# Fewer chunks scattered whole, and every third node one-hot on ScalarE, in a graph update with two segment sums

## What is computed

```python
in_agg = segment_sum(edge_feat, dst, 6250)          # edge_feat: 200000 x 64
out_agg = segment_sum(edge_feat, src, 6250)
h = relu(concatenate([in_agg, out_agg, x], 1) @ W1 + b1)   # W1: 192 x 256
out = layernorm(x + h @ W2 + b2)                    # W2: 256 x 64
```

## Time and profile before

| | |
|---|---|
| median of 3 runs | 1354.76 us (1354.26 to 1355.96) |
| profiled execution | 1358.4 us |
| its span, first to last instruction | 1356.6 us |
| mean granted TensorE clock | 0.942 |
| busy: PE, weight load, DVE, ACT, POOL | 83%, 68%, 86%, 68%, 80% of the span |
| scatters (L775) | 628, 1.673 us mean |
| node one-hots on DVE, on ACT | 1300, 260 |

### The profile page before, as it was taken

One profiled execution on the slowest core, in us unless ns is written; L12 is line 12 of the kernel. 1 busy time (PEld: TensorE's weight loads), 2 busy tenths in 40 slices (PEclk: granted clock), 3 DMA queues, 4 the chain that ended last, 5 costly groups with the idle time before them and its releaser, 6 DMA issues.

```text
span 1356.6 us, 60124 instructions
## 1 busy us (share of the span) xinstructions
PE 1129.9 (83%) x21795; PEld 917.9 (68%) x21795; DVE 1167.1 (86%) x3489; ACT 926.2 (68%) x2047; POOL 1084.1 (80%) x663
## 2 busy tenths in 40 slices
PE   2667588988898888898888889989888898899596
PEld 2546377877787777787777767767666676777443
DVE  6756689988999999998899989999879898999486
ACT  6233588988898888888788876666566676666242
POOL 3888888888888888888888888888888888888533
PEclk9976789999999999999899989999989998999798
DMA  9332489999998899998999998889878887888441
GB/s 300 49 43 17 62 182 209 212 195 199 203 215 203 200 202 205 209 210 199 207 235 243 241 217 210 199 209 216 212 166 209 192 200 188 185 195 207 79 133 45
DMA packets 251312, 247.53 MB, mean 182 GB/s; under 512 B 105587, under 2 KB 213460, under 8 KB 250966
## 3 DMA queue, kind: packets, MB, share of 16 engines
q1 hardware_dynamic: 158632, 216.16, 52.4%
q0 software_dynamic: 92384, 28.77, 27.8%
q10 hardware_dynamic: 144, 0.48, 0.1%
HBM read 139.12 MB, written 106.21 MB: 181 GB/s over the span
## 4 chain that ended last, share of the span: by engine, by line
POOL 33%; DMA 26%; issue 23%; PE 11%; DVE 4%; ACT 2%; SPq 1%; POOLq 0%; ACTq 0%; DVEq 0%
POOL out_tables L775 32%; DMA out_tables<-payload,target 23%; PE psum L1679 3%; DMA feat<-in_edge_attr 2%; PE psum L1890 2%; PE psum L1845 1%; PE psum L1902 1%; PE psum L1655 1%; ACT slots_out L870 1%; DMA rows_i<-in_dst 1%; PE psum L1618 1%; DVE same L1357 1%; PE psum L1628 0%; ACT parts L849 0%; ACT payload L887 0%
## 5 line engine op out<-in xcount | busy, mean ns | idle before, releaser
L775 POOL DMA_INDIRECT out_tables<-payload,target x628 | 1050.7, 1673 | 209.4 <-issue 170.0
L1679 PE MATMUL psum<-parts,to_slot 128*128 128x194 bf16 x4524 | 457.9, 251 | 88.7 <-ACT slots_out L870 75.0
L1679 PEld LDWEIGHTS psum<-parts,to_slot 128*128 128x128 bf16 x4524 | 377.9, 99 | 136.1 <-ACT slots_out L870 92.6
L870 ACT ACTIVATE slots_out<-psum 128x388 bf16<-128x388 f32 x780 | 341.7, 499 | 68.4 <-PE psum L1679 54.2
L1703 PE MATMUL psum<-to_node,slots_in 64*64 64x313 bf16 x9360 | 353.3, 301 | 24.6 <-issue 19.9
L1703 PEld LDWEIGHTS psum<-to_node,slots_in 64*64 64x64 bf16 x9360 | 278.2, 108 | 85.4 <-issue 33.4
L1291 DVE TENSOR_SCALAR to_slot<-iota_h,slot 128x480 bf16<-128x480 f16 (+1 forms) x936 | 291.3, 367 | 29.6 <-PE psum L1679 29.1
L1330 DVE TENSOR_SCALAR to_node<-iota_h,slot_rel 128x318 bf16<-128x318 f16 x780 | 239.7, 329 | 0.0
L1330 DVE TENSOR_SCALAR to_node<-iota_rows,slot_rel 128x318 bf16<-128x318 f16 x520 | 181.8, 350 | 0.0
L887 ACT ACTIVATE payload<-psum 128x256 f32<-128x256 f32 x157 | 58.9, 375 | 159.5 <-PE psum L1757 87.1
L937 ACT ACTIVATE apart<-iota_h,slot_rel 128x318 bf16<-128x318 f16 x260 | 131.9, 551 | 12.0 <-DVE slot_rel L1302 10.3
(11 more groups left out here) (138 smaller groups left out, 894.6 us busy)
## 6 DMA issues: line engine op xcount, KB each, us to landing
slot_tiles<-slots_out SPq DMA_DIRECT2D x156, 388.0 KB
feat<-in_edge_attr SPq DMA_DIRECT2D x195, 256.0 KB
slots_in<-slot_tiles SPq DMA_DIRECT2D x152, 242.5 KB
slots_in<-slot_tiles SPq DMA_DIRECT2D x152, 230.4 KB
slot_tiles<-slots_out SPq DMA_DIRECT2D x78, 194.0 KB
out_tables<-payload,target POOLq DMA_INDIRECT x628
out_tables<-zeros POOLq DMA_DIRECT2D x4, 1600.0 KB
feat<-out_tables SPq DMA_DIRECT2D x48, 128.0 KB, 2.3
```

The source lines that it names most:

```text
L775: e.indirect_dma_start(out_tab, at, payload[b][:, t, :], None, element_offset=k * TABLE_ROWS * D, compute_op=ALU.add).then_inc(s_tab[k], 16)
L870: e.activation(slots_out[b][:, g:g + n, m, :], round_bank(b, r)[:, 0:n * SLOT_W].rearrange("p (g w) -> p g w", w=SLOT_W), ACT.Copy).then_i ...
L1679: last = e.matmul(round_bank(b, r)[:, o:o + SLOT_W], to_slot[m][:, COLUMN_FROM[k] + t * P:COLUMN_FROM[k] + (t + 1) * P], parts[b][:, SHARE ...
```

## The change

- SUMS 16 to 14: 80 chunks are shared, 14 go whole after them; 160 tiles per node pair, 1600 in all. The units 1 to 12 have 118.3 tiles each, the last has 160.
- ROUND 6 to 3: tiles 2, 5, 8, ... are ACT's. Its second pass (`from_far`) covers two tiles, whose `to_node` buffers are three apart, in one instruction; APARTS 4.
- `slots_in` in a ring of 6 parts of 16 tiles, PARTS = 10, no longer a multiple of the ring.
- In the summing units the targets of the first quad are worked out apart, after quad 1's "same node", so that POOL can start on them.
- `in_group` in six pieces, one per k, each waiting for the one before.

```diff
-SUMS = 16
+SUMS = 14
...
-RING = 4
-PARTS = 2 * RING
+RING = 6
+PARTS = 10
...
-ROUND = 6
+ROUND = 3
 BY_SCALAR = 1
 BY_VECTOR = ROUND - BY_SCALAR
-APARTS = 2
+APARTS = 4
...
-            return isinstance(c, int) and c in (0, END_SHARE)
+            return isinstance(c, int) and (c == 0 or END_SHARE <= c < N_CHUNKS)
...
+        def ring_buf(g, p):
+            return (g * PARTS + p) % RING
...
-            def from_far(g, i):
-                n = scalar_rounds(tile_no(g, i)) - 1
-                e.wait_ge(s_apart, n + 1)
-
-                e.wait_ge(s_tile, tile_no(g, i) + 1)
-                e.activation(to_node[:, node_buf(g, i), :], apart[:, n % APARTS, :], ACT.Relu, bias=1.0,
-                             scale=-1.0).then_inc(s_to_node_act, 1)
+            def from_far(tiles):
+                first, last = tiles[0], tiles[-1]
+                n = scalar_rounds(tile_no(*first)) - 1
+                e.wait_ge(s_apart, n + len(tiles))
+
+                e.wait_ge(s_tile, tile_no(*last) + 1)
+                e.activation(to_node[:, node_buf(*first):node_buf(*last) + 1:ROUND, :], apart[:, n % APARTS:n % APARTS + len(tiles), :],
+                             ACT.Relu, bias=1.0, scale=-1.0).then_inc(s_to_node_act, len(tiles))
...
-                    for k in range(0, len(mine), APARTS):
-                        for at in mine[k:k + APARTS]:
-                            to_far(*at)
-                        for at in mine[k:k + APARTS]:
-                            from_far(*at)
+                    pairs = []
+                    for at in mine:
+                        odd = (scalar_rounds(tile_no(*at)) - 1) % 2
+                        if odd and pairs and len(pairs[-1]) == 1 and not at[1] < pairs[-1][0][1]:
+                            pairs[-1].append(at)
+                        else:
+                            pairs.append([at])
+                    for k in range(0, len(pairs), APARTS // 2):
+                        for pair in pairs[k:k + APARTS // 2]:
+                            for at in pair:
+                                to_far(*at)
+                        for pair in pairs[k:k + APARTS // 2]:
+                            from_far(pair)
...
-                step(e.tensor_tensor(in_group[:, :, :, :], from_group[:, :, 0:SLOT_GROUPS, :], from_group[:, :, 1:, :],
-                                     ALU.subtract))
+                for k in range(MINI):
+                    last = e.tensor_tensor(in_group[:, k, :, :], from_group[:, k, 0:SLOT_GROUPS, :], from_group[:, k, 1:, :],
+                                           ALU.subtract)
+                    if k < MINI - 1:
+                        last.then_inc(s_in_group, 1)
+                        e.wait_ge(s_in_group, (MINI - 1) * n + k + 1)
+                step(last)
...
                     if q == 1:
                         for h in range(HALVES):
                             add_window(c, b, ats, h)
+                        targets(c, b, c, mode, (0, QUAD))
...
-                        targets(c, b, c, mode)
+                        targets(c, b, c, mode, (QUAD, mode.cols))
```

More of the change, by code:

```diff
@@ L326, in build @@
         s_from_group = sem("s_from_group")
+        s_in_group = sem("s_in_group")
         s_masked = sem("s_masked")
@@ L445, in targets_no @@
                 return c + 1 + (1 if c > 0 else 0)
-            return c + (2 if mode is SHARING else 3)
+            if mode is SHARING:
+                return c + 2
+            return c + 2 + (c - END_SHARE if mode.sums else SUMS)
         def quad_buf(q, b, mode):
@@ L622, in load_tiles @@
                 lo = PART_FROM[p]
-                into = slots_in[p % RING][:, a - lo:z - lo, :].rearrange("p t w -> p (t w)")
+                into = slots_in[ring_buf(g, p)][:, a - lo:z - lo, :].rearrange("p t w -> p (t w)")
                 homes = slot_rows[0:HOME_AT[MINI], :].rearrange("(k r) w -> r k w", k=MINI)
@@ L627, in load_tiles @@
                     e.dma_start(into[j:P:LOADS, :], homes[both * g:both * (g + 1), 2 * j:2 * j + 2, a * SLOT_W:z * SLOT_W]
-                                ).then_inc(s_slot_in[p % RING], 16)
+                                ).then_inc(s_slot_in[ring_buf(g, p)], 16)
                 at = HOME_AT[MINI] + shared * g
                 e.dma_start(into[LOADS - 1:P:LOADS, :], slot_rows[at:at + shared, a * SLOT_W:z * SLOT_W]
-                            ).then_inc(s_slot_in[p % RING], 16)
+                            ).then_inc(s_slot_in[ring_buf(g, p)], 16)
             def load_part(g, p):
@@ L936, in to_far @@
                 k = i - PART_FROM[p]
-                e.activation(apart[:, n % APARTS, :], iota_h[:, 0:HOT], ACT.Abs, bias=slot_rel[p % RING][:, k:k + 1],
+                e.activation(apart[:, n % APARTS, :], iota_h[:, 0:HOT], ACT.Abs, bias=slot_rel[ring_buf(g, p)][:, k:k + 1],
                              scale=-1.0).then_inc(s_apart, 1)
-            def from_far(g, i):
-                n = scalar_rounds(tile_no(g, i)) - 1
-                e.wait_ge(s_apart, n + 1)
-                e.wait_ge(s_tile, tile_no(g, i) + 1)
-                e.activation(to_node[:, node_buf(g, i), :], apart[:, n % APARTS, :], ACT.Relu, bias=1.0,
-                             scale=-1.0).then_inc(s_to_node_act, 1)
+            def from_far(tiles):
[5 more added lines that the diff above has]
+                             ACT.Relu, bias=1.0, scale=-1.0).then_inc(s_to_node_act, len(tiles))
             def tiles_to_nodes(u, q):
@@ L1297, in relative @@
             def relative(g, p):
-                e.wait_ge(s_slot_in[p % RING], 16 * LOADS * (g * (PARTS // RING) + p // RING + PIECES))
+                e.wait_ge(s_slot_in[ring_buf(g, p)], 16 * LOADS * ((g * PARTS + p) // RING + PIECES))
                 e.nop(nofuse=True)
                 n = PART_FROM[p + 1] - PART_FROM[p]
-                e.scalar_tensor_tensor(slot_rel[p % RING][:, 0:n], slots_in[p % RING][:, 0:n, 3 * D],
-                                       pair_first[:, bass.ds(g, 1)], slots_in[p % RING][:, 0:n, 3 * D + 1],
+                e.scalar_tensor_tensor(slot_rel[ring_buf(g, p)][:, 0:n], slots_in[ring_buf(g, p)][:, 0:n, 3 * D],
+                                       pair_first[:, bass.ds(g, 1)], slots_in[ring_buf(g, p)][:, 0:n, 3 * D + 1],
                                        ALU.subtract, ALU.add).then_inc(s_slot_rel, 1)
@@ L1329, in tiles_to_nodes @@
                         hot, numbers = hot.rearrange("p (a k) -> p a k", k=HOT // HOT_ROW), iota_rows[:, :, 0:HOT_ROW]
-                    e.tensor_scalar(hot, numbers, slot_rel[p % RING][:, k:k + 1], None, ALU.is_equal).then_inc(s_to_node, 1)
+                    e.tensor_scalar(hot, numbers, slot_rel[ring_buf(g, p)][:, k:k + 1], None, ALU.is_equal).then_inc(s_to_node, 1)
             def targets(c, b, d, mode, columns=None):
@@ L1703, in product @@
                     return e.matmul(ps_groups[g % 2][h][cols, 0:GROUP_NODES],
-                                    slots_in[p % RING][rows, j - PART_FROM[p], D * k:D * (k + 1)],
+                                    slots_in[ring_buf(g, p)][rows, j - PART_FROM[p], D * k:D * (k + 1)],
                                     to_node[rows, node_buf(g, j), 0:GROUP_NODES], start=(j == 0 and k < 2), stop=(j >= TILES - 2 and k == 2))
```

## The result

| | before | after |
|---|---|---|
| median | 1355.36 us (4 runs, 1354.26 to 1360.93) | 1395.32 us (4 runs, 1389.4 to 1408.93) |
| profiled execution | 1358.4 us | 1389.4 us |
| span | 1356.6 us | 1387.6 us |
| scatters; node one-hots on DVE, on ACT | 628; 1300, 260 | 604; 1067, 533 |

The change makes the kernel slower: ratio 1.031, 95% interval 1.026 to 1.036. The forecast was 1377 us, slower with a chance of 0.86.

The account below looks back on a forecast made before the run. POOL bounds the kernel thinly before and ACT after; a later unit 1, twelve units of 37.0 us and a 42.0 us last unit put the first layer 22 us later: 1358.4 + 22 - 3.6 = 1377 us; range 1357 to 1407.

Parts of the forecast that it names:

- POOL stops being the bound, ACT becomes it: Summing units: ACT's doubled share of one-hots makes it 36.2 us busy, units 37.0 us, above POOL's 30.6; chance 0.75.
- The merged pass: ACT's second pass over two tiles at once: 0.63 us in all, giving 0.76 us per ACT tile instead of 0.81.
- PE's pace: Summing units: 19.4 more tiles each make PE 31.6 us busy, 33.7 us with its own gaps.
- rival A: Summing units: PE, not ACT, is the bound if an ACT tile costs 0.67 us or less; 1335 us, chance 0.10.
- Sharing and early stage: Before the summing units: two more shared chunks cost 16.1 us, in_group in six pieces saves 3.0 us.
- The last unit: End of the summing stage: ACT's 148 tiles take 37.5 us, 42.0 with evictions, ending at 1304.2 us.
- The end of the stage: After PE's last tile: + 3.1 us to the folded sums, first layer on the sums at about 1307.8 us.
- From the profiled execution to the median: Whole kernel: the profiled execution was taken as 3.6 us above the median, so 3.6 us were subtracted.
- B: Summing units: PE works in bursts at a lower granted clock and sets the pace at 39 us; 1407 us, chance 0.12.
- C: ACT's second pass: pairs don't form in some quads, below 0.3 us per unit, inside the forecast; no separate chance.
- D: Whole kernel: the terms cancel at 1355 us, needing 1.8 us less per unit than forecast; chance 0.03.
- The ring: Summing stage: six parts instead of four reach DVE earlier, but DVE is no bound, so worth nothing.

Follow-up runs that it names:

- every_sixth: The changed kernel with every sixth node one-hot on ACT instead of every third; 1338.6 us, 0.989 of the kernel before.
- sixth_in_group_whole: The changed kernel with every sixth node one-hot on ACT and the in_group subtraction in one piece; 1326.6 us, 0.979 of the kernel before.
- second_pass_single: The changed kernel with ACT's second pass over one tile at a time, as before the change; 1411.8 us, 1.040 of the kernel before.

## Why the prediction was right, and what was mis-sized

**POOL stops being the bound, ACT becomes it.** Right, and the profile shows each step of it: ACT 97.5% busy, units of 36.7 us (37.0 forecast), ACT 35.8 us busy per unit (36.2), PE 31.2 (31.6), DVE 28.5 (some 27, 1.5 too low, which cost nothing as DVE had slack). Runs show the cause: take ACT's share back and units fall to 32.4 us, price its second pass higher and they rise by that price.

**The merged pass.** It was in no row and was taken from two other groups at 0.63 us from one beginning to the next; 0.62 was measured (1.25 us for two). The share of 0.76 us per tile is exact.

**PE's pace, too high.** I gave PE 31.6 us busy and 2.1 of gaps, 33.7 per unit. every_sixth has the same tiles per unit, and there PE is 364.72 / 12 = 30.4 us busy in units of 32.35 us. So PE needs at most 32.35. It didn't matter here, where ACT is fuller, but rival A stood on it.

**Sharing and early stage.** 16.1 - 3.0 was forecast for the two chunks and in_group; unit 0 began at 808.8 us in place of 790.9, + 17.9. The mark of chunk 82, which was unit 0 before, shows how it divides:

```profile
791.52 0.55 DVE L1299 TENSOR_TENSOR onehot<-rel,iota_twice 128x768 bf16<-128x768 bf16 x1
```

The two chunks took the 17.3 us from there to 808.8 (16.1 forecast), and up to there nothing was gained (+ 0.6 us where I had - 3.0). Unit 0 itself was to be 2.5 us longer for its ACT tiles and was not: 11.3 us against 11.7. So unit 1 began at 820.2 (818.2 forecast), close because an error of + 4.8 us met one of - 2.8, which is luck. DVE's timeline has the first six pieces in one row, 6.12 us for all of them against 5.03 for the one (5.15 in sixth_in_group_whole, which subtracts 9600 columns as the changed kernel does); POOL's shows the scatters beside the second six:

```profile
49.13 6.12 DVE L1228 TENSOR_TENSOR in_group<-from_group 128x1600 bf16<-128x1600 bf16 x6
```

```profile
112.66 2.31 POOL L781 DMA_INDIRECT out_tables<-payload,target  x1 [0.30 <-issue]
115.27 1.75 POOL L781 DMA_INDIRECT out_tables<-payload,target  x1 [0.30 <-issue]
117.32 1.75 POOL L781 DMA_INDIRECT out_tables<-payload,target  x1 [0.30 <-issue]
...
1173.38 1.58 POOL L781 DMA_INDIRECT out_tables<-payload,target  x1 [6.20 <-DVE target L1358]
```

The excess over 1.55 us is 0.76 + 0.20 + 0.20 us for these three, where the one long scatter lost 3.8. So POOL gets some 2.6 us back there for 1.1 us more of DVE, and the sharing stage's first scatter began at 165.8 us in place of 168.2. By chunk 82 that lead was gone, and the one piece in sixth_in_group_whole costs no lead at all (166.6 us, as in every_sixth). At 1173.38 the same timeline shows what POOL does in the summing stage: 6.2 us idle until the rest of the targets come.

**The last unit: the term that was too small.** I laid 42 us from the last one-hot to PE's last tile; it took 49.1 (1261.10 to 1310.2). The work itself was priced well: ACT evicts the unit's first payload at 1267.84 and is done with its tiles and sums at 1309.2, 41.3 us. But I put that work at the one-hot's mark, as if ACT stood where DVE stands. Where ACT is the bound it is behind: DVE makes the window's one-hot of a unit while ACT still has 6.7 us of the unit before. That is the largest error of the sum, + 7 us. The distance from the one-hot to ACT's first payload was 5.9 to 7.8 us in every one of the units 1 to 13, so it didn't matter for their length, only once, at the end. (Of the 42 us, 4.5 for the evictions came from no row; the 41.3 measured bear them out.)

**The end of the stage.** From PE's last tile to the first L1911 I had 3.6 us, 3.1 of them from rows; the chain of waits shows 6.2:

```profile
1300.21 9.99 PE psum L1724 x271
...
1314.21 0.86 issue
1315.07 0.42 PE psum L1903 x2
1315.95 0.44 DVE aggT L1565
1316.43 5.40 PE psum L1911 x8
```

PE's tiles end at 1310.2, then come its own-feature products, the folds, and only after them the turning of the tables' sums (L1903), which stand behind them in PE's program. Before, PE was done with its products and folds at 1270 us and waited 13.7 us for the tables, which waited for POOL's last scatter, so the interval that I took ended at the folded sums and had next to nothing for the turning and DVE's addition of what is turned (L1565), which take from 1314.2 to 1316.4 us. + 2.6 us.

With the last unit's mark 1 us early (1261.1 against 1262.2) that makes the first L1911 at 1316.4 against 1307.8, and the profiled execution 1389.4 us against 1380.4: 9.0 us.

**From the profiled execution to the median.** The rest of the 18 us. I took the profiled execution to be 3.6 us above the median, as before the change. After it, it was the fastest of four, 5.9 us below. One offset from one pair of numbers was too little to build on: the executions of one kernel with 80 shared chunks lie over 2 to 20 us. Between the profiled ones the largest differences arose in the sharing stage; the others have no trace that could show where. Half of the 18 us is thus this offset and not the mechanism, and that the sum itself was only 9 us off owes something to the errors that cancelled before unit 1.

**The rivals.** A's condition (0.67 us per tile or less) wasn't met. Its price, 1335 us, was close to what every sixth gave, partly by luck: its units of 33.7 us were at least 1.35 too long. B, the clock: PE's granted clock was 0.98 in units 1 to 12, so nearly all at 2.4 GHz, though PE's weight loads waited 38.7 us for ACT there and PE rested 5.5 us per unit ((440.9 - 374.7) / 12). In second_pass_single it was 0.95, and still ACT and not PE was the full one. So B fell. Why the clock held isn't shown. My reading of the unit from 977 us was off: the 7.3 us there are ACT's wait, and PE's own longest rest in it was 2.5 us,

```profile
985.75 0.24 PE L1755 MATMUL psum<-parts,same 128*128 128x65 bf16 x1 [2.49 <-ACT again_sign L888]
```

while its longest in units 1 to 12 of the changed kernel was 2.4 us. B's price was also summed wrongly: 39 us per unit are 2.0 more than 37.0, not 2.5, so 12 x 2.0 gives 1401 us. The range's upper end of 1407 stood on that; the next bound below it was 1403, and the 1395.3 measured lie under all three. C: 40 single second passes in twelve units, 3.3 per unit at 0.05 us each, inside the forecast. D, that the terms cancel, fell with the measured time.

**What I costed at nothing.** The ring: no run tries it where ACT is the bound; where DVE is, a unit is about 1 us shorter with six parts. The early targets: nothing that can be seen in either.

## A version that beats both

The change with every sixth one-hot left on ACT: 1338.6 and 1335.7 us in two timings, 0.989 (0.983 to 0.995) and 0.987 (0.983 to 0.990) of the kernel before, and some 4% under the changed one. The gain is small, but all eight kernels with 80 shared chunks and every sixth or every fourth one-hot on ACT lie at 0.979 to 0.990. The kernel before with SUMS = 14 and no other edit, 1340.2 us, is the simplest, and by the medians only 1.6 and 4.5 us behind these two timings. Every fourth is not better: DVE is relieved, but PE, at 30.5 us per unit and with gaps of its own, is as full.

## What to carry to other kernels

When work is moved to an idle engine, add up that engine's time per unit of work after the move and put it beside the pace that the old bound gives; idle by 35% doesn't mean room for a doubled share of an operation that costs there three times as much. Here leaving the share at one in six, as it was, and taking only the two chunks' scatters off POOL gave the gain. And a sum laid from marks of one engine needs the distance of the new bound from these marks, once, at its end.

## What was not expected of the hardware

- The early stage's six pieces of the subtraction took 6.12 us against 5.03 (5.15 for as many columns), and each scatter beside them lost 0.2 to 0.8 us, where one piece cost one scatter 3.8 us.
- The mark that ends the sharing stage lay from 805.0 to 821.2 us in the twelve profiled executions with 80 shared chunks, whose work up to there is nearly the same.
- PE's granted clock stayed at 0.98 in units 1 to 12 of the changed kernel, with PE busy 85% and never at rest for more than 2.4 us; in the unit before the change with a longest rest of 2.5 us it was 0.86 at 83%. What makes the difference isn't shown.
